# A decoder layer whose three parts become one block: barriers, early loads and unlimited scatters

## The reference

```python
def layer(x, c):
    h = layernorm(x)                      # self-attention, 16 heads of 64, causal, with a position bias
    q, k, v = heads(h @ Wq), heads(h @ Wk), heads(h @ Wv)
    s = (q @ k.T + causal + pos_bias) / 64
    x = x + merge(softmax(s) @ v) @ Wo + bo
    h = layernorm(x)                      # cross attention, 16 heads of 16
    q = rms_norm(heads(h @ xWq.T + bq), q_gamma)
    k, v = split(heads(c @ xWkv.T + bkv)) # interleaved
    k = rms_norm(k, k_gamma)
    x = x + merge(softmax(q @ k.T / 4) @ v)
    h = layernorm(x)                      # experts: 32 routed, 8 that return their input
    p = softmax(h @ cls.T)                # 40 scores
    top = top_k(p + score_bias, 6)
    w = 2.5 * p[top]
    out = h * sum(w of the 8 zero experts)
    for e in range(32):
        gate, up = split(h @ gate_up[e].T)
        out += w[e] * ((silu(gate) * up) @ down[e].T)
    return x + out
```

## Time and profile before

| | us |
|---|---|
| median of 3 runs | 1418.47 (1417.62 to 1419.89) |
| profiled execution, whole | 1413.1 |
| its span, first to last instruction | 1411.4 |

### The profile page before, as it was taken

One profiled execution on the slowest core, in us unless ns is written; L12 is line 12 of the kernel. 1 busy time (PEld: TensorE's weight loads), 2 busy tenths in 40 slices (PEclk: granted clock), 3 DMA queues, 4 the chain that ended last, 5 costly groups with the idle time before them and its releaser, 6 DMA issues. The chain is left out here.

```text
span 1411.4 us, 27027 instructions
## 1 busy us (share of the span) xinstructions
PE 1225.4 (87%) x8240; PEld 731.3 (52%) x8240; DVE 770.5 (55%) x2639; ACT 824.4 (58%) x1678; POOL 697.7 (49%) x778
## 2 busy tenths in 40 slices
PE   6999999999999566999899999998896139999975
PEld 4666766776775454433343334333221128888853
DVE  6675566466556186461255025525530268888867
ACT  5666456456556035679867976797896015555530
POOL 2776576567557103455055415531556357555550
PEclk9999999999999987999999999999998559999998
DMA  7976466466455121010011001001322596555549
GB/s 248 334 251 223 171 229 227 167 227 214 160 173 193 63 78 32 16 33 16 3 47 32 16 2 47 5 29 52 114 96 92 227 342 189 170 168 170 169 150 386
DMA packets 148181, 196.21 MB, mean 139 GB/s; under 512 B 13088, under 2 KB 134576, under 8 KB 147008
## 3 DMA queue, kind: packets, MB, share of 16 engines
q1 hardware_dynamic: 137280, 164.08, 35.2%
q0 software_dynamic: 10752, 30.26, 5.9%
HBM read 71.59 MB, written 122.70 MB: 138 GB/s over the span
## 5 line engine op out<-in xcount | busy, mean ns | idle before, releaser
L1349 ACT ACTIVATE xa_probs<-xa_banks 128x1024 f32<-128x1024 f32 (+1 forms) x416 | 402.0, 1045 | 100.8 <-PE xa_banks L1202 99.9
L327 POOL TENSOR_SCALAR sa_probs<-sa_probs,sa_recip 128x128 f32<-128x128 f32 (+3 forms) x256 | 274.9, 1087 | 176.3 <-DVE sa_recip L581 176.1
L460 ACT ACTIVATE sa_probs<-sa_probs,sa_neg_max 128x128 f32<-128x128 f32 (+3 forms) x256 | 141.9, 555 | 148.2 <-DVE sa_neg_max L518 148.1
L1217 PE MATMUL xa_banks<-xa_probs,xa_v_one 128*17 128x512 f32 (+1 forms) x1664 | 221.3, 604 | 6.8 <-ACT xa_q_aug L1297 4.5
L1202 PE MATMUL xa_banks<-xa_q_aug,xa_k_aug 32*128 32x512 f32 (+1 forms) x1664 | 155.0, 446 | 21.2 <-issue 9.9
L1870 POOL DMA_INDIRECT parts<-mo_y,mo_dest x128 | 122.7, 959 | 78.1 <-DVE mo_dest L2121 69.8
L518 DVE CUSTOM_DVE_ANT_0 sa_probs<-sa_ps,sa_toeplitz 128x128 f32<-128x128 f32 (+3 forms) x256 | 115.4, 487 | 38.2 <-PE sa_ps L390 35.4
L1917 PE MATMUL mo_banks<-mo_w_all,mo_xs_t 128*128 x512 | 133.5, 384 | 0.0
L1202 PEld LDWEIGHTS xa_banks<-xa_q_aug,xa_k_aug 32*128 32x128 f32 (+1 forms) x1664 | 62.3, 182 | 115.0 <-ACT xa_probs L1349 77.8
L578 DVE COPY sa_pt<-sa_ptr 128x128 f32<-128x128 f32 (+3 forms) x128 | 62.7, 490 | 104.0 <-PE sa_ptr L401 103.9
L1014 POOL DMA_INDIRECT rows<-xa_k_area,xa_place_i x72 | 70.0, 972 | 65.2 <-DMA rows<-xa_k_area,xa_place_i 37.6
(11 more groups left out here) (307 smaller groups left out, 2373.4 us busy)
## 6 DMA issues: line engine op xcount, KB each, us to landing
rows<-sa_blank SPq DMA_DIRECT2D x128, 548.0 KB, 3.7
mo_xs<-rows SPq DMA_DIRECT2D x128, 137.0 KB, 2.2
parts<-sa_blank SPq DMA_DIRECT2D x96, 128.0 KB, 3.9
mo_w_all<-parts SPq DMA_DIRECT2D x16, 768.0 KB, 15.1
mo_w_all<-in_gate_up_p SPq DMA_DIRECT2D x4, 2048.0 KB, 20.0
xa_raw<-in_ctx_t SPq DMA_DIRECT2D x24, 256.0 KB, 2.8
sa_toeplitz<-extended_bias SPq DMA_DIRECT2D x8, 512.0 KB, 7.6
mo_w_all<-in_down_p SPq DMA_DIRECT2D x4, 1024.0 KB, 21.7
```

The costliest lines, as they stand in the source:

```text
L327: pool.tensor_scalar(probs[:, t % SLOTS, 0:w], probs[:, t % SLOTS, 0:w], recip[:, col:col + 1], None, ALU.mult).then_inc(probs_ready, 1)
L460: act.activation(probs[:, t % SLOTS, 0:w], probs[:, t % SLOTS, 0:w], ACT.Exp, bias=neg_max[:, i:i + 1], scale=-1.0, accum_out=sums[:, i:i ...
L1217: last = pe.matmul(banks[32 * i:32 * i + XD + 1, 6 + group % 2, :], v_one[b % 2][0:m, c, 4 * g + i, :], probs[0:m, (2 * j + i // 2) % RING ...
L1349: act.activation(probs[0:m, n % RING, :, :], banks[0:m, 2 * (n % 3):2 * (n % 3) + 2, :], ACT.Exp).then_inc(probs_ready, 1)
```

## The change

All three parts are now written into one block. Each function returns a program per engine, and `layers` calls them one after another, so every engine goes on to the next part by itself. The barriers are gone; waits for the events that matter take their place. Reuse of SBUF between parts is arranged by the order of allocation, and all semaphores live to the end. Further:

- the loads of cross attention's prologue, the halves of weights and context and the first layernorm are called from within self-attention (`first_loads`, `first_halves`, `first_norm`);
- two thirds of the experts' first matrices are loaded in the last batch of cross attention, and POOL builds the expert part's constants in the batch before (`more_consts`);
- the last batch's x2 stays in SBUF (`kept.x_sb`) instead of being stored and loaded;
- `send` has no limit on transfers in flight; the scatters of `y` get one of 8, and so do the loads of `parts`;
- 12 of the last batch's 24 row scatters are interleaved with the scatters of the first 12 tiles.

The core of the diff, without the changes of indentation:

```diff
 def self_attention
+    LOADS_AT = STEPS * B - 5
+    HALVES_AT = STEPS * B + 3
+    NORM_AT = STEPS * B + 5
 # sync, in the loop over s, ahead of the loads and stores of x
+                if s == LOADS_AT:
+                    weights_used(sp)
+                    first_loads(sp)
 # vector, in the loop over s, behind the copy of ot
+                if s == HALVES_AT:
+                    first_halves(dve)
+                if s == NORM_AT:
+                    first_norm(dve)
-        nc.all_engine_barrier(sems_to_clear=range(sems[0].num, sems[-1].num + 1))
+        def weights_used(eng):
+            eng.wait_ge(fill_psum, fill_at["k", B - 1, PAIRS - 1] + 1)
+        def finished(eng):
+            eng.wait_ge(fill_psum, len(what))
+            eng.wait_ge(fill_out, dve_out[-1])
+            eng.wait_ge(x1_out, 16 * B)
+            eng.wait_ge(filled, 16 * (STEPS * B + 1 + TILES * TOP_K))
+        def psum_left(eng):
+            eng.wait_ge(fill_out, dve_out[-1])
 def cross_attention
-    IN_FLIGHT = 2
+    WEIGHTS_AT = (B - 1, 21)
+    MORE_CONSTS_AT = (B - 2, 44)
 # sync: all before load(sp, 0, 2) is first_loads
-                        if b >= 1 and s == min(STORE_AT, len(slots_of(b)) - 1):
+                    if 1 <= b < B and s == STORE_AT:
+                    if (b, s) == WEIGHTS_AT:
+                        sp.wait_ge(pv_done, (B - 1) * SLOTS)
+                        first_weights(sp)
-                sp.wait_ge(x2_out, 16 * B)
-                sp.wait_ge(xr_out, 16 * ROUTED)
-                for landed in sent:
-                    sp.wait_ge(landed, 16 * ROUTED * TT * TOP_K // IN_FLIGHT)
 # gpsimd
-                    if n >= IN_FLIGHT:
-                        pool.wait_ge(sent[n % IN_FLIGHT], 16 * (n // IN_FLIGHT))
-                        in_=packed[:, t, :], in_offset=None).then_inc(sent[n % IN_FLIGHT], 16)
+                    in_=packed[:, t, :], in_offset=None).then_inc(sent[0], 16)
+            finished(pool)      # ahead of the memset of v_one
+                    if (b, s) == MORE_CONSTS_AT:
+                        more_consts(pool)
 # tensor, ahead of run(-1, False)
-                pe.wait_ge(const_ready, 3)
+            psum_left(pe)
+            pe.wait_ge(const_ready, 2)
 # scalar, behind the first high halves
+            finished(act)
-        nc.all_engine_barrier(sems_to_clear=range(sems[0].num, sems[-1].num + 1))
+        def through(eng):
+            eng.wait_ge(x2_part, QUADS * B)
+        def stored(eng):
+            eng.wait_ge(xr_out, 16 * ROUTED)
 def experts
+    SCATTERS = 8
+    SUM_LOADS = 8
-    LOADS = 4
+    ALONE = 12
+    FIRST_WEIGHTS = 22
+        def load_weights(sp, lo, hi):
+            at, n = lo * KD * 2 * INTER, (hi - lo) * KD * 2 * INTER
+            sp.dma_start(w_all[:, at:at + n], gate_up_p[:, at:at + n]).then_inc(w_in, 16)
+        def first_weights(sp):
+            load_weights(sp, 0, FIRST_WEIGHTS // 2)
+            load_weights(sp, FIRST_WEIGHTS // 2, FIRST_WEIGHTS)
+        def parts_landed(eng, t):
+            eng.wait_ge(parts_in[t % SUM_LOADS], 16 * (t // SUM_LOADS + 1))
+        def tile_landed(eng, t):
+            eng.wait_ge(y_sent[t % SCATTERS], 16 * (t // SCATTERS + 1))
+        def run_sync(sp):
+            kept.through(sp)
+            load_weights(sp, FIRST_WEIGHTS, E_ROUTED)
 # then two loads of down_p
+            kept.stored(sp)
 # then the load of acc
+            sp.wait_ge(sent[0], 16 * SENT_BEFORE)
                 sp.wait_ge(steer_ready, 1)
 # the loads of parts
+                if t >= SUM_LOADS:
+                    parts_landed(sp, t - SUM_LOADS)
 # gpsimd
+        def send_tile(pool, t):
+            if t >= SCATTERS:
+                tile_landed(pool, t - SCATTERS)
                     pool.wait_ge(own_ready, t + 1)
                     pool.wait_ge(y_ready, t + 1)
 # gpsimd, in the loop over the 24 scatters of rows
+                if n >= ALONE:
+                    send_tile(pool, n - ALONE)
 # vector
-                dve.wait_ge(x_in, 16)
+            kept.through(dve)
+            kept.stored(dve)
                 layernorm(dve, chain, packed[:, :, 0:D], own_x, TT, stats, mean_var, var[:], rstd[:], tmp[:]
                           ).then_inc(xn_ready, 1)
+            dve.wait_ge(const_ready, 2)
+            dve.tensor_copy(counted[:, 0, :], picked[:].bitcast(F32))
+            dve.tensor_copy(meta[:, :, 2, :], spare_no[:])
+def layers
+        with nc.Block() as block:
+            @block.sync
+            def _(sp):
+                own.sync(sp, first_loads)
+                cross.sync(sp, first_weights)
+                mixed.sync(sp)
```

More of the change, by code:

```diff
@@ L11 @@
 import math
+from collections import namedtuple
 from contextlib import ExitStack
@@ L845, in cross_attention @@
         row_ready = sem("row_ready")
-        sent = [sem(f"sent{i}") for i in range(IN_FLIGHT)]
         xr_done = sem("xr_done")
@@ L1657, in experts @@
+        def through(eng):
+            eng.wait_ge(x2_part, QUADS * B)
+        def stored(eng):
+            eng.wait_ge(xr_out, 16 * ROUTED)
+        return (Programs(run_sync, run_gpsimd, run_tensor, run_scalar, run_vector), first_loads, first_halves,
+                first_norm, Kept(x_sb, cls, bias_row, router_in, through, stored))
+def experts(nc, held, kept, sent, x2, gate_up_p, down_p, rows, parts, picked, out):
     SENTINELS = 2
@@ new lines, in layers, with _ @@
+def layers(nc, x, wq, wk, wv, wo, bo, bias_rev, ext_scratch, x1, rows, parts, ctx_t, xwq_t, xbq, xwkv_t,
+           xbkv, q_gamma, k_gamma, x2, cls_t, score_bias, picked, sent, gate_up_p, down_p, out):
+    with ExitStack() as held:
+        own, weights_used, finished, psum_left = self_attention(
+            nc, held, x, wq, wk, wv, wo, bo, bias_rev, ext_scratch, x1, rows, parts)
+        cross, first_loads, first_halves, first_norm, kept = cross_attention(
+            nc, held, finished, psum_left, x1, ctx_t, xwq_t, xbq, xwkv_t, xbkv, q_gamma, k_gamma, x2, cls_t,
+            score_bias, rows, picked, sent)
+        mixed, first_weights, more_consts = experts(
+            nc, held, kept, sent, x2, gate_up_p, down_p, rows, parts, picked, out)
+        with nc.Block() as block:
[4 more added lines that the diff above has]
+                mixed.sync(sp)
+            @block.gpsimd
+            def _(pool):
+                own.gpsimd(pool)
+                cross.gpsimd(pool, more_consts)
+                mixed.gpsimd(pool)
+            @block.tensor
+            def _(pe):
+                own.tensor(pe)
+                cross.tensor(pe)
+                mixed.tensor(pe)
+            @block.scalar
+            def _(act):
+                own.scalar(act)
+                cross.scalar(act)
+                mixed.scalar(act)
+            @block.vector
+            def _(dve):
+                own.vector(dve, first_halves, first_norm)
+                cross.vector(dve)
+                mixed.vector(dve)
```

2856 lines of the change are left out of this document (1424 added, 1432 removed).

## The result

| | before | changed |
|---|---|---|
| median in the first comparison, us | 1418.05 | 1374.07 |
| profiled execution, us | 1413.1 | 1373.6 |
| its span, us | 1411.4 | 1371.9 |

The ratio is 0.9699 (95% interval 0.9671 to 0.9726). Two later comparisons of the same two kernels, on two chips, gave 0.9692 (0.9659 to 0.9725; 1415.27 and 1373.64) and 0.9718 (0.9688 to 0.9748; 1416.28 and 1376.58). So the change is worth 40 to 44 us where the kernel before takes 1415 to 1418 us; 1373.8 was forecast. On two other chips the kernel before takes 1440 us, and there parts of the change cost time; the whole change was never run on one of them.

The account below looks back on a forecast made before the run. Within each part one engine is nearly always busy, so only the two seams between parts were in question. Terms -14.0 - 27.7 - 3.0 = -44.7 took 1413.1 to 1368.4; plus 5.4 gave 1373.8 us, range 1366 to 1389.

Parts of the forecast that it names:

- First seam: Self-attention to cross attention: TensorE starts behind the last sum, prologue work done early; -14.0 us, bounds -10.6 and -15.
- rival c: First seam: the prologue gives back its lead because a later wait decides; only -10.6, 1377.2 us; chance 0.12.
- some 2 us: End of self-attention: the early layernorm delays VectorE's first output sum by this much, unnoticed by TensorE thanks to a second bank.
- The scatters and the second seam: End of cross attention: scatters every 1.26 us, layernorm reads SBUF without store, barrier and load; -27.7 us, bounds -25.9 and -10.8.
- Rival (b): Cross attention's scatters don't get faster, from port locks or descriptors queued behind weights: 1390.7 us; chance 0.15 including a partial case.
- port lock: Scatters: VectorE's two-port operations shut GpSimd out of descriptor writes; 17.8 us would come back if each scatter took the longest.
- Router and first tile: Layernorm to first tile: router chain unchanged at 33.7 us, tile's load no longer queued behind others; -3.0 us, bounds 0 and -3.2.
- First tile's load 5.5 to 2.5: Start of the tiles: VectorE sees the first tile 2.2 plus 0.3 us after its issue instead of 5.5.
- Tiles and the end: Expert tiles to kernel end: TensorE still sets 1.64 us a tile, added waits cost nothing; 0, bounds -1 and +2.
- profiled execution to median: Whole kernel: the median of timed runs lies 5.4 us above the profiled execution, added to 1368.4.
- likeliest case: Whole kernel: the terms hold as summed, 1373.8 us, own range 1369 to 1378; chance 0.66.
- (b) to (f): Scatters not faster 0.15, prologue lead lost 0.12, POOL bounds tiles 0.02, change ineffective 0.02, more gain from TensorE's clock 0.03.

Follow-up runs that it names:

- late prologue: Changed kernel with cross attention's first loads, halves and layernorm called behind self-attention, still without a barrier: 1490.94 us, 1.0366 of the kernel before.
- limit of four: Changed kernel with at most four scatters in flight in the last batch of cross attention: 1382.65 us, 0.9757 of the kernel before.
- late weights: Changed kernel with the first 22 experts' matrices loaded behind the last head sum, not in the last batch: 1471.54 us, 1.0237 of the kernel before.
- limits of two: Changed kernel with the rows' scatters of the first three batches again two at a time: 1432.27 us, 0.9964 of the kernel before.
- third piece: Changed kernel with third and fourth context pieces loaded before the last x1 store, ScalarE released by VectorE's last sum: 1375.78 us, 0.9713 of the kernel before.
- second late prologue: Changed kernel with cross attention's early loads, halves and layernorm again called behind self-attention, on another chip: 1490.02 us, 1.0340 of the kernel before.

## Why the prediction was right, point by point

**First seam, -14.0.** Measured 13.65 at the subtraction and still 13.3 at the last copy of o. The mechanism held in each step: start behind the last sum, SP and ScalarE released at 486.1 to 486.3, ScalarE's copy at 489.85 (489.5 forecast), and only 0.3 given back later (rival c). VectorE made the first output sum 2.2 us late (471.96 to 474.15), forecast "some 2 us", and TensorE's 64 products of the projection took 14.05 us as before. One row was read too widely: VectorE is idle 3.03 us before three of the four output sums and 4.05 before the first, which changes nothing here. Of the 13.65 the barrier and the block's end are 1.05; the rest is the early work and its order. With the barrier gone and the order on VectorE as the late prologue had it, the first exponentials came at 564.89, later than the 559.08 of the kernel before (without the limit, which acts only later) on the same chip.

**The scatters and the second seam, -27.7.** Measured 27.8, of which POOL's queue is 16.8 (16.9 forecast: 1103.0 less 1086.1). The last head sum ended at 1072.90 where the sum of both terms gives 1072.1. Alone, in the kernel before, taking the limit away gave 14.4 us (1416.28 to 1401.90), and the interval of the ratio is 10 to 18 us, so it takes in the 16.9. In that run's trace the last head sum ends 3.1 us behind the start of the last copy of o, where the two traces of the kernel before have 19.9 and 18.0: 16.8 or 14.9 us. That trace also has TensorE's half clock between 463 and 470 us, before the scatters begin (last section), so a part of what is missing from 16.9 may be that. The round trip of store, barrier and load (11.0 us) was never undone alone; it is read from the traces. Rival (b) named something real: "descriptors queue up behind the 5.8 MB" is what the limit of four met (7.4 us at the last head sum). The changed kernel escapes it since POOL doesn't wait. On the port lock, the Trainium skill ("SBUF — State Buffer", the box "The DVE blocks DMA trap") says that GpSimd can't write descriptors while VectorE runs an operation of that mode. The 72 took 70.5 us, a mean of 0.979 against a median of 0.960 and a longest of 1.43: 1.4 us in all above the median. The trace doesn't show whether VectorE held those few.

**Router and first tile, -3.0.** The router's chain took 33.4 us (33.7 before), and the whole term gave 1.4 us (42.5 less 41.1). The step that was mis-sized: "First tile's load 5.5 to 2.5" is true for VectorE (-3.1), but TensorE needs three tiles' rows before its first product, and gained 1.1 there (from row_no 9.0 before, 7.9 now).

**Tiles and the end, 0, bounds -1 and +2.** Measured +3.1, outside its bounds: 0.8 in the tiles (last y 41.75 earlier, first product 42.5), and 2.35 at the last scatters. The second is the stop of 3.03 us in front of tile 124's scatter. Its y was ready at 1322.8, the eighth scatter before it was done (DMA share 0.00 from 1325 to 1327), so it is not the added limit of eight. It stands at the same tile in all nine traces of the changed kernel and its variants, and the kernel before has its own stop of 3.06 us at tile 113, with 14 tiles left to catch up; in the changed kernel three are left.

**The two errors that cancel.** In the profiled executions the change gave 1413.1 - 1373.6 = 39.5 us, where the terms sum to 44.7. To that sum the text added 5.4 us for "profiled execution to median". For the changed kernel this was 0.4. The profiled execution of before was simply a short one (medians of the three comparisons: 1418.05, 1415.27, 1416.28). So 1373.8 met 1374.07 with 5 us too much gain and 5 us too high an offset. The range and the likeliest case stand by mechanism, the last digit doesn't.

**The rivals.** None of (b) to (f) happened where both kernels ran. Missing among them was the chip: on two of them, with scatters issued back to back, ScalarE stood still for up to 16.5 us at a time and TensorE for up to 8.4.

## What to carry to other kernels

A barrier can be cheap in itself (1 us at the first boundary, 3.7 us of waits for TensorE's queue at the second); the larger cost is the work that could have been issued ahead of it (12.6 of 13.65 us at the first). Moving that work without minding the order on each engine gave it all back: without the barrier, the late prologue was 5.8 us behind the kernel before. A small limit on transfers in flight is paid twice, in each landing and where other traffic delays the landings, but on two chips the kernels without it were the ones whose other engines stood still; measure an unlimited queue on more than one chip. Add a profile-to-median offset only if it is seen in several executions. And before you put a shift of a few us down to an edit, compare the granted clock of the stretches ahead of it.

## What the runs showed of the hardware that was not expected

- Two kinds of chip for one program. Two chips ran the kernel before in 1439 and 1441 us, the others in 1415 to 1418. On the former, without a limit, ScalarE's exponentials wait for nothing that the trace shows, 54 to 58 us in total and up to 16.5 us at once (five traces), while POOL issues scatters back to back; with two in flight it is 5.5 us in total. The packets of the instruction queues are few in such stretches (in the late weights kernel from 1018 to 1043 one of queue q8 and none of q14; in the changed kernel from 1030 to 1055 two and two), which would fit engines that lack instructions. But engines that stand also fetch less, so this isn't shown as the cause. It stays open, and so does what differs between the chips. The tiles are longer there too: 234.7 us from the first scatter of y to the last with two in flight (1154.23 to 1388.89), 208.3 in the changed kernel elsewhere (1121.70 to 1329.98).
- POOL stops at fixed places of its program, whatever the chip: in the changed kernel and its variants at tiles 89, 101 (100 in two of them) and 124, by about 1.6, 1.0 and 3.0 us; in the kernel before, with and without the limit, at 89 and 113, by 1.34 and 3.06 (the chips of 1440 us have others besides). In the changed kernel at all three tiles, and in the kernel before at 113, y and its destinations were ready and the eighth scatter before had long been issued. Where such a stop falls decided 2.3 us here.
- TensorE's granted clock near the end of self-attention differs between executions. Between about 463 and 470 us it is 0.50 (1.2 GHz) in seven traces: the limits of two and of four, late weights, the third piece, the second late prologue, and two of the three without the limit in the kernel before. It is 1.00 (2.4 GHz) in the other seven, among them all three of the changed kernel and both of the kernel before. Ahead of it, from 460 to 462, the engine was busy 0.66 us of the two in three of the traces that fell (third piece, limit of four, the last one without the limit) and 0.66 to 0.84 in those that didn't. At half clock the last products with the values took 4.53 us in place of 2.37, and the first exponentials of the four variants of the changed kernel came at 546.9 to 547.7 instead of 544.6 to 545.1. The edits don't decide it: three of these four act 400 us later, and both the late prologue and the kernel before without the limit, each one program run on several chips, show it at 0.50 in one trace and at 1.00 in another. What decides it is open.
